# Hyperbolic attention and FP8 feed-forward: a register for the exponential's scale, a small exponential one slot later, and another order of VectorE's steps

## The chip, the cores and the metric

One core of a Trainium2 chip runs the whole layer. The metric is the device time of one execution in microseconds, the median of several runs. TensorE multiplies, ScalarE evaluates functions, VectorE does the elementwise work and reads the products out of PSUM, SyncE (SP) issues all transfers in the stretch in question.

## The reference

The input x has 8 sequences of 1024 tokens with 256 features. The first half of the layer is attention with 16 heads of 16 features, whose weights come from distances in the Poincare ball:

```python
q_h, k_h, v_h = exp_map_at_origin(x @ W.T per head, c)
diff = |q|^2 - 2 q.k + |k|^2
denom = max((1 - c |q|^2) * (1 - c |k|^2), EPS)
dist = arccosh(max(1 + 2 c diff / denom, 1 + EPS)) / sqrt(c)
weights = softmax(-beta_pos * dist - attention_bias)
out = weights @ log_map_at_origin(v_h)      # then exp map, log map, @ W_o.T, + x
```

The second half normalises the sum, quantises it to FP8 (e4m3), multiplies by a 256x256 matrix, adds a bias and adds the result to the sum.

## The kernel before

**Tiles.** The 8192 tokens are 16 groups (`NG`) of 512 queries. A group takes 32 steps: 4 sets of four heads (`HG`) by 8 blocks of 128 keys (`KT`). That makes N = 512 steps, written out without loops. A step is four heads x 128 keys x 512 queries, a tile of 128x2048. In units of four steps (`UNIT`) the kernel chooses between two forms by a flag that it has computed on the chip: closed or open. All engines but TensorE and SP branch on it at each unit's start (L912 to L920, L1008 to L1018). An open unit is one in which the bound of `denom` can be above EPS; the inputs give three open units, which begin at steps 164, 276 and 492.

**A step, closed.** TensorE writes the distances of step n+1 to four PSUM banks (`distances`, in two halves; the tiles of successive steps share two banks, so the second half waits for `freed`). ScalarE takes the logarithm of the four banks into `U` (`log`, L881), which frees the banks, and then the exponential of the step before in place (`power`, L888), whose scale is `g.NEGB`, a column of 128 equal values in SBUF. TensorE multiplies it with the values of its keys (`values`, PSUM bank 6, summed over 8 steps), two steps after the distances. `U` has four slots (`RING`).

**A step, open.** VectorE first writes the bound into `U` (`bound`, L941, four instructions of 128x512), multiplies it with the distances from PSUM (`clamp`, L950, 128x2048, signals `freed`), and ScalarE takes the logarithm of `U` in place (L876). VectorE does the product of step n at the head of step n and the bound of step n+1 behind it; only then follow its copies and slot work of step n.

**Bank 7.** All other matmuls share one PSUM bank in a fixed order (`Uses`): each use waits until VectorE has copied the one before (`b7_copied`), each copy waits for its matmuls (`b7_filled`). Projections of later groups (`PROJECT_USES`: X transposes of the input, M the projection to q, k and v, R transposes of the finished rows, A a maximum for the flag) and the finish of earlier ones (`FINISH_USES`: T, W the output projection, Q, Y the FP8 product) have slots; slot k of the projection is step k - 4 of a group, slot k of the finish is step k. A use marked BOTH is divided: TensorE does one half before `values` of the step and one behind; its copy is in the second half of the step (`in_step(G, s, 1)`). Step 3 to 9 and 11 of a group have M0 to M7; 12 and 13 have T0 and T1, 14 and 15 have W0 and W1. S (step 2, 10, 18, 26) transposes the sums. In a step without a use TensorE does two products for nothing (`keep_busy`, L833). At the end of 8 steps VectorE copies bank 6 to `OTs` (`copy_sums`, L956) and signals `ot_done`, for which the next `values` that starts a sum waits.

**Slot work.** `project.vector` and `finish.vector` are VectorE's elementwise work by slot, at the end of a step. Slot 18 ends with `nrm` (L446). ScalarE's part of it is one small exponential over 128x128 (L407 to L410), now at slot 19: it waits for `n_rdy` and stands behind `log(n)` and `power(n - 1)` of step 15, the last of a unit. Slot 20 of VectorE begins with a wait for its result (`e_rdy`); at step 16 `copy_sums` stands ahead of it. The first two groups are projected before the steps begin, the third from step 0 on, so the steps hold 14 such exponentials.

Each engine's order is the order of the code. TensorE in step n: second half of `distances(n + 1)`, first half of `distances(n + 2)`, uses, `values(n - 1)`, uses.

Of the kernel before, what the change touches and what calls it, by code (L numbers as in the profile page):

```python
# [7 lines left out]
ACT = mybir.ActivationFunctionType  # L8
# [3 lines left out]
I32 = mybir.dt.int32  # L12
# [29 lines left out]
UNIT = 4  # L42
RING = 4
# [50 lines left out]
def hold(eng, passed):  # L94
    eng.sem_inc(passed, 1)
# [167 lines left out]
def at(table, slot, half):  # L263

    return [key for key, where in table.items() if where == (slot, half) or (half, where) == (1, (slot, BOTH))]
# [13 lines left out]
def project_stage(nc, ctx, g, a, uses):  # L279
# [125 lines left out]
            v.sem_inc(a.open_rdy, 1)  # L405

    def scalar(act, n, k):  # L407
        if k == 19:
            act.wait_ge(n_rdy, n + 1)
            act.activation(e[:, :, :], nrm[:, :, :], ACT.Exp, scale=g.M2SC).then_inc(e_rdy, 1)  # L410

# [231 lines left out]
def emit_layer(nc, g):  # L643

    with ExitStack() as ctx:
        def sb(name, shape, dt=F32):
            return _sb(nc, ctx, name, shape, dt)
# [7 lines left out]
        U = sb("U", [P, RING, HPG, GTOK])  # L655
# [14 lines left out]
        def in_step(G, s, half):  # L670

            found = []
            if s % KT == SUM_STEPS % KT and half == 0:
                x = HG * G + (s - SUM_STEPS) // KT
                if 0 <= x < NG * HG and G < NG:
                    found.append(("S", x // HG, x % HG))
            found += [(kind, n, i) for n, k in finished(G, s) for kind, i in at(FINISH_USES, k, half)]
            found += [(kind, n, i) for n, k in projected(G, s) for kind, i in at(PROJECT_USES, k, half)]
            return found

        def projected(G, s):

            return [(n, k) for n, k in ((G + 2, s + EARLY), (G + 3, s + EARLY - STEPS))
                    if n < NG and 0 <= k < PROJECT_SLOTS]

        def finished(G, s):

            return [(n, k) for n, k in ((G - 2, s + STEPS), (G - 1, s)) if n >= 0 and 0 <= k < FINISH_SLOTS]
# [4 lines left out]
        def before_steps(k):  # L693

            return [(n, k - lag) for n, lag in enumerate(LAGS) if 0 <= k - lag < PROJECT_SLOTS]
# [27 lines left out]
        def split(n):  # L723

            return n // STEPS, (n % STEPS) // KT, n % KT
# [5 lines left out]
        def place(n, h):  # L731

            return (h + 2) % HPG if n % 2 else h

        def chunk(n):
            return g.ps[:, 2 * (n % 2):2 * (n % 2) + 4, :].rearrange("p b n -> p (b n)")

        def opened(n):

            G, hg, kt = split(n)  # L740
            return (G * 2 + kt // UNIT) * HG + hg

        def flags_of(n):

            G, hg, kt = split(n)
            return max(G, 2 * (G // 2) + kt // UNIT) + 1

        with nc.Block() as block:
# [120 lines left out]
            @block.scalar  # L869
            def _(act):  # L870
                act.preload_act_table_set(ACT_SET)

                def log(n, is_open):
                    if is_open:
                        act.wait_ge(freed, n + 1)
                        act.activation(U[:, n % RING], U[:, n % RING], ACT.Ln, scale=-2.0, bias=1.0).then_inc(ln_open, 1)  # L876
                    else:
                        act.wait_ge(d_rdy, n + 1)
                        if n >= RING:
                            act.wait_ge(pv_done, n - RING + 1)  # L880
                        act.activation(U[:, n % RING].rearrange("p b n -> p (b n)"), chunk(n), ACT.Ln,  # L881
                                       scale=-2.0 / EPS, bias=1.0).then_inc(freed, 1)

                def power(n, *logs):

                    for done in logs:
                        act.wait_ge(done, n + 1)
                    act.activation(U[:, n % RING], U[:, n % RING], ACT.Exp, scale=g.NEGB).then_inc(exp_done, 1)  # L888

                def unit(n0, is_open):  # L890
                    if is_open:
                        if n0:
                            power(n0 - 1, freed, ln_open)
                    for n in range(n0, n0 + UNIT):
                        G, s = n // STEPS, n % STEPS
                        if is_open and n > n0:
                            power(n - 1, ln_open)
                        log(n, is_open)
                        if not is_open and n > n0:
                            power(n - 1, freed)  # L900
                        elif not is_open:
                            if n0:
                                power(n0 - 1, freed, ln_open)
                            act.sem_inc(ln_open, UNIT)
                        for m, k in projected(G, s):
                            project.scalar(act, m, k)

                act.activation(past[:, :], g.NEGB, ACT.Exp, scale=math.log(2.0 * U_EXACT + 1.0)).then_inc(past_rdy, 1)
                for k in range(LEAD):
                    for n, slot in before_steps(k):  # L910
                        project.scalar(act, n, slot)
                for n0 in range(0, N, UNIT):  # L912
                    o = opened(n0)
                    act.wait_ge(a.open_rdy, flags_of(n0))
                    hold(act, passed_act)
                    is_open = act.value_load(a.opens[0:1, o:o + 1], min_val=0, max_val=1)
                    with act.If(is_open > 0):
                        unit(n0, True)
                    with act.Else():
                        unit(n0, False)  # L920
                power(N - 1, freed, ln_open)

            @block.vector
            def _(v):
# [10 lines left out]
                def bound(n):  # L935

                    G, hg, kt = split(n)
                    if n >= RING:
                        v.wait_ge(pv_done, n - RING + 1)
                    for h in range(HPG):  # L940
                        ins = v.tensor_scalar(U[:, n % RING, place(n, h), :], rqb[:, h, :],  # L941
                                              a.rk[:, (G // 2) % 2, hg * HPG + h, kt:kt + 1],
                                              1.0 / EPS, ALU.mult, ALU.min)
                    ins.then_inc(m_rdy, 1)

                def clamp(n):
                    v.wait_ge(m_rdy, n + 1)
                    v.wait_ge(d_rdy, n + 1)
                    all4 = U[:, n % RING].rearrange("p b n -> p (b n)")
                    v.tensor_tensor(all4, all4, chunk(n), ALU.mult).then_inc(freed, 1)  # L950
# [25 lines left out]
                def copy(kind, n, i):  # L976
                    if kind == "S":
                        normalise(n, i)
                    elif (kind, i) in FINISH_USES:
                        finish.copy(v, n, (kind, i))  # L980
                    else:
                        project.copy(v, n, (kind, i))

                def unit(n0, is_open):
                    for n in range(n0, n0 + UNIT):
                        G, s = n // STEPS, n % STEPS
                        if is_open:
                            clamp(n)
                            if n + 1 < n0 + UNIT:
                                bound(n + 1)  # L990
                        for key in in_step(G, s, 0):
                            copy(*key)
                        if n % KT == 0 and n >= KT:
                            copy_sums(n // KT - 1)
                        for key in in_step(G, s, 1):
                            copy(*key)
                        for m, k in finished(G, s):
                            finish.vector(v, m, k)
                        for m, k in projected(G, s):
                            project.vector(v, m, k)  # L1000
# [7 lines left out]
                for n0 in range(0, N, UNIT):  # L1008
                    o = opened(n0)
                    v.wait_ge(a.open_rdy, flags_of(n0))  # L1010
                    hold(v, passed_v)
                    is_open = v.value_load(a.opens[0:1, o:o + 1], min_val=0, max_val=1)
                    with v.If(is_open > 0):
                        v.wait_ge(rqb_in, 16 * (n0 // KT + 1))
                        bound(n0)
                        unit(n0, True)
                    with v.Else():
                        v.sem_inc(m_rdy, UNIT)  # L1018
                        unit(n0, False)
# [266 lines left out]
```

## Time and profile before

| | us |
|---|---|
| median of 3 runs | 2226.95 |
| the three runs | 2231.99, 2209.66, 2226.95 |
| the profiled execution | 2226.39 |
| its span, first to last instruction | 2224.1 |
| TensorE busy | 1855.3 |
| ScalarE busy | 1896.5 |
| VectorE busy | 1172.3 |

The mean granted TensorE clock is 0.951 of 2.4 GHz. The profile comes from one execution; its own time lies 0.6 us under the median. Successive instructions of an engine can overlap a little, so the pitch (start to start) is the measure of what an instruction costs in a row of others; the duration is longer. Ends of matmuls are modelled. The last group of stretches holds the three open units up to the second closed step behind each, and 11 us around a step 17. In the rows, PE is TensorE, ACT is ScalarE, DVE is VectorE; a bracket gives the idle time of the engine before the instruction and what ended it.

### The profile page before, as it was taken

The page shows a single profiled execution, that of the slowest core. Times are in us where ns is not written, and L with a number is a line of the kernel's source. Part 1 is how long each engine was busy: PE and PEld are TensorE (multiplying, and loading weights), DVE is VectorE, ACT ScalarE, POOL GpSimd, SP SyncE. Part 2 cuts the span into 40 slices and gives each one's busy share as a digit, 9 for nine tenths or more (in the row PEclk, how much of TensorE's full clock was granted, in tenths as well). Part 3 has the DMA queues.
Part 4 walks back from the last instruction along what each step waited for, and adds up shares of the span by engine and source line. Part 5 has one row for each costly group of instructions (what it writes and reads, how often), then busy time and mean ns, then how long its engine had stood idle before and what let it go on. Part 6 is the DMA issues. An engine that isn't in the chain of part 4 may idle for free. (4 is left out here: it accounts for less than half of the span.)

```text
span 2224.1 us, 29561 instructions
## 1 busy us (share of the span) xinstructions
PE 1855.3 (83%) x10721; PEld 617.0 (28%) x10721; DVE 1172.3 (53%) x2869; ACT 1896.5 (85%) x1055; POOL 2.6 (0%) x15
## 2 busy tenths in 40 slices
PE   4459898998989859898989789898989898899792
PEld 2222222232322213222222222222222223233221
DVE  5563345555555545556555655555565555423335
ACT  1019999989999949999999699999999999999790
POOL 0000000000000000000000000000000000000000
PEclk9969999989999969999999899999999999999895
DMA  1031220313131211312213031312213031311000
GB/s 40 22 111 48 80 69 20 120 39 120 39 101 39 99 40 39 103 37 91 67 56 103 19 120 39 101 39 91 67 39 115 25 110 39 110 39 58 20 20 30
DMA packets 112937, 142.54 MB, mean 64 GB/s; under 512 B 35676, under 2 KB 61533, under 8 KB 112733
## 3 DMA queue, kind: packets, MB, share of 16 engines
q1 hardware_dynamic: 112732, 140.13, 20.1%
q8 instruction: 90, 1.47, 0.3%
q14 instruction: 115, 0.93, 0.2%
HBM read 85.07 MB, written 55.05 MB: 63 GB/s over the span
## 5 line engine op out<-in xcount | busy, mean ns | idle before, releaser
L888 ACT ACTIVATE U<-U,sc 128x2048 f32<-128x2048 f32 x512 | 1047.6, 2048 | 0.3
L881 ACT ACTIVATE U<-ps 128x2048 f32<-128x2048 f32 x500 | 959.8, 1920 | 63.6 <-PE ps L797 57.7
L797 PE MATMUL ps<-q_T,k_T 18*128 18x512 f32 x4096 | 638.8, 655 | 183.3 <-ACT U L881 132.7
L810 PE MATMUL ps<-U,vals 128*32 128x512 f32 x4096 | 564.9, 624 | 50.3 <-ACT U L888 42.6
L797 PEld LDWEIGHTS ps<-q_T,k_T 18*128 18x128 f32 x4096 | 200.4, 188 | 406.5 <-ACT U L881 318.1
L347 PE MATMUL ps<-wT,xnT 128*128 128x384 f32 x512 | 247.8, 574 | 17.1 <-DVE qkv L373 14.3
L373 DVE COPY qkv<-ps 128x384 f32<-128x384 f32 x128 | 71.3, 557 | 260.0 <-PE ps L347 259.9
L833 PE MATMUL ps<-woT,ident 128*128 128x256 f32 x428 | 157.9, 452 | 0.0
L956 DVE COPY OTs<-ps 128x512 f32<-128x512 f32 x64 | 44.3, 692 | 194.9 <-PE ps L810 173.4
L352 PE MATMUL ps<-ident,rows 128*128 128x128 f32 x512 | 110.3, 315 | 44.1 <-DVE rows L482 29.8
L347 PEld LDWEIGHTS ps<-wT,xnT 128*128 128x128 f32 x512 | 83.9, 202 | 222.9 <-issue 119.7
L810 PEld LDWEIGHTS ps<-U,vals 128*32 128x32 f32 x4096 | 81.6, 109 | 228.9 <-ACT U L888 192.1
L410 ACT ACTIVATE e<-nrm,sc 128x128 f32<-128x128 f32 x16 | 6.4, 402 | 140.7 <-DVE nrm L446 140.7
L833 PEld LDWEIGHTS ps<-woT,ident 128*128 128x128 f32 x428 | 67.0, 197 | 184.4 <-issue 177.6
L352 PEld LDWEIGHTS ps<-ident,rows 128*128 128x128 f32 x512 | 57.1, 150 | 210.2 <-issue 148.3
L381 DVE COPY q_T<-ps 128x512 f32<-128x512 f32 x64 | 44.1, 690 | 108.0 <-PE ps L352 107.8
L383 DVE COPY k_T<-ps 128x512 f32<-128x512 f32 x64 | 44.3, 692 | 86.0 <-PE ps L352 85.9
L546 PE MATMUL ps<-woT,fi_ocT 128*128 128x256 f32 x256 | 78.1, 432 | 1.6 <-DVE fi_ocT L568 0.8
L876 ACT ACTIVATE U<-U 128x2048 f32<-128x2048 f32 x12 | 22.9, 1912 | 58.8 <-DVE U L950 58.8
L964 DVE TENSOR_REDUCE den<-ps 128x16 f32<-128x256 f32 x64 | 27.2, 425 | 87.0 <-PE ps L819 86.5
L546 PEld LDWEIGHTS ps<-woT,fi_ocT 128*128 128x128 f32 x256 | 47.3, 205 | 58.4 <-issue 29.8
L438 DVE TENSOR_REDUCE ss<-sqr 128x48 f32<-128x768 f32 x64 | 61.0, 953 | 2.2
(164 smaller groups left out, 1168.9 us busy)
## 6 DMA issues: line engine op xcount, KB each, us to landing
rqb<-q_scratch SPq DMA_DIRECT2D x64, 1024.0 KB, 5.6
q_scratch<-q_T SPq DMA_DIRECT2D x16, 1024.0 KB, 4.5
k_scratch<-k_T SPq DMA_DIRECT2D x16, 1024.0 KB, 6.8
v_scratch<-vals SPq DMA_DIRECT2D x16, 768.0 KB, 9.2
xt<-in_L_attn_x_dram SPq DMA_DIRECT2D x16, 512.0 KB, 6.2
fi_xt<-in_L_attn_x_dram SPq DMA_DIRECT2D x16, 512.0 KB, 5.7
out_dram<-fi_x SPq DMA_DIRECT2D x16, 512.0 KB, 4.1
rk_scratch<-rk SPq DMA_DIRECT2D x16, 32.0 KB, 11.9
```

Of the source, the lines that this page charges most:

```text
L347: ins = pe.matmul(bank[:, 0:384], xnT[:, dc, t * P:(t + 1) * P], g.wT[:, dc, half * 384:(half + 1) * 384], start=dc == 0, stop=dc == 1)
L352: ins = pe.transpose(bank[:, t * P:(t + 1) * P], rows[:, qk, t, hg * HPG:(hg + 1) * HPG, :].rearrange("p h r -> p (h r)"), g.ident[:, :])
L373: v.tensor_copy(qkv[:, t, 24 * half:24 * (half + 1), :].rearrange("p h d -> p (h d)"), bank[:, 0:384]).then_inc(a.b7_copied, 1)
L383: v.tensor_copy(a.k_T[:, b % 2, hg, u * GTOK:(u + 1) * GTOK], bank).then_inc(a.b7_copied, 1)
L438: step(v.tensor_reduce(ss[:, t, :], sqr[:, :].rearrange("p (h d) -> p h d", d=DH), AX.X, ALU.add))
L546: ins = pe.matmul(bank[:, a * D:(a + 1) * D], ocT[:, dc, t * P:(t + 1) * P], g.woT[:, dc, :], start=dc == 0, stop=dc == 1)
L797: ins = pe.matmul(g.ps[:, 2 * pair + i, :], a.k_T[HB * h:HB * h + RD, b % 2, hg, kt * P:(kt + 1) * P], a.q_T[HB * h:HB * h + RD, G % 3, hg ...
L810: ins = pe.matmul(g.ps[HB * h:HB * h + VW, 6, :], a.vals[:, b % 2, kt, (hg * HPG + h) // 2, DH * (h % 2):DH * (h % 2) + VW], U[:, n % RING ...
L833: pe.matmul(g.ps[:, 7, 0:D], g.ident[:, :], g.woT[:, 0, :], start=True, stop=True)
L881: act.activation(U[:, n % RING].rearrange("p b n -> p (b n)"), chunk(n), ACT.Ln, scale=-2.0 / EPS, bias=1.0).then_inc(freed, 1)
L888: act.activation(U[:, n % RING], U[:, n % RING], ACT.Exp, scale=g.NEGB).then_inc(exp_done, 1)
L956: v.tensor_copy(OTs[:, :], g.ps[:, 6, :]).then_inc(ot_done, 1)
```

## The change

It does four things. The small exponential moves from slot 19 to slot 20, in ScalarE's order one `log` and one `power` later. The scale of the large exponential is loaded once into a register of ScalarE and given to the instruction from there, instead of as a column of SBUF. In an open unit VectorE does bound and product of step n+1 at the head of step n, ahead of all copies and slot work of step n; the first product of the unit stands in front of the loop. In every unit `copy_sums` moves behind the copies of the second half of the step. One branch of ScalarE's `unit` is written otherwise and gives the same order.

```diff
--- before.py
+++ after.py
@@ -405,7 +405,7 @@
             v.sem_inc(a.open_rdy, 1)
 
     def scalar(act, n, k):
-        if k == 19:
+        if k == 20:
             act.wait_ge(n_rdy, n + 1)
             act.activation(e[:, :, :], nrm[:, :, :], ACT.Exp, scale=g.M2SC).then_inc(e_rdy, 1)
 
@@ -869,6 +869,8 @@
             @block.scalar
             def _(act):
                 act.preload_act_table_set(ACT_SET)
+                exponent = act.alloc_register("exponent")
+                act.reg_load(exponent, g.NEGB[0:1, :].bitcast(I32))
 
                 def log(n, is_open):
                     if is_open:
@@ -885,12 +887,11 @@
 
                     for done in logs:
                         act.wait_ge(done, n + 1)
-                    act.activation(U[:, n % RING], U[:, n % RING], ACT.Exp, scale=g.NEGB).then_inc(exp_done, 1)
+                    act.activation(U[:, n % RING], U[:, n % RING], ACT.Exp, scale=exponent).then_inc(exp_done, 1)
 
                 def unit(n0, is_open):
-                    if is_open:
-                        if n0:
-                            power(n0 - 1, freed, ln_open)
+                    if is_open and n0:
+                        power(n0 - 1, freed, ln_open)
                     for n in range(n0, n0 + UNIT):
                         G, s = n // STEPS, n % STEPS
                         if is_open and n > n0:
@@ -898,7 +899,7 @@
                         log(n, is_open)
                         if not is_open and n > n0:
                             power(n - 1, freed)
-                        elif not is_open:
+                        if not is_open and n == n0:
                             if n0:
                                 power(n0 - 1, freed, ln_open)
                             act.sem_inc(ln_open, UNIT)
@@ -984,16 +985,15 @@
                 def unit(n0, is_open):
                     for n in range(n0, n0 + UNIT):
                         G, s = n // STEPS, n % STEPS
-                        if is_open:
-                            clamp(n)
-                            if n + 1 < n0 + UNIT:
-                                bound(n + 1)
+                        if is_open and n + 1 < n0 + UNIT:
+                            bound(n + 1)
+                            clamp(n + 1)
                         for key in in_step(G, s, 0):
+                            copy(*key)
+                        for key in in_step(G, s, 1):
                             copy(*key)
                         if n % KT == 0 and n >= KT:
                             copy_sums(n // KT - 1)
-                        for key in in_step(G, s, 1):
-                            copy(*key)
                         for m, k in finished(G, s):
                             finish.vector(v, m, k)
                         for m, k in projected(G, s):
@@ -1013,6 +1013,7 @@
                     with v.If(is_open > 0):
                         v.wait_ge(rqb_in, 16 * (n0 // KT + 1))
                         bound(n0)
+                        clamp(n0)
                         unit(n0, True)
                     with v.Else():
                         v.sem_inc(m_rdy, UNIT)
```

## Rows read from the trace of the kernel before

**Rows 1.** The page, part 1: busy time of each engine over the span.
```profile
PE 1855.3 (83%) x10721; PEld 617.0 (28%) x10721; DVE 1172.3 (53%) x2869; ACT 1896.5 (85%) x1055; POOL 2.6 (0%) x15
```

**Rows 2.** Line 881, the closed logarithm: ns min/median/max, first and last start in us.
```profile
L881 ACT ACTIVATE U<-ps x500: 1864/1906/2072, 156.1 to 2163.1; 128x2048 f32<-128x2048 f32 x167
```

**Rows 3.** The waits: waiting line, releaser: us in total, times, longest.
```profile
ACT e L410 <- DVE nrm L446: 140.7, 15, 57.2
...
ACT U L881 <- PE ps L797: 57.7, 39, 27.2
```

**Rows 4.** Timeline of a plain step: start, us, engine, line, what.
```profile
1003.03 1.87 ACT L881 ACTIVATE U<-ps 128x2048 f32<-128x2048 f32 x1
...
1004.79 2.00 ACT L888 ACTIVATE U<-U,sc 128x2048 f32<-128x2048 f32 x1
...
1004.96 1.24 PE L797 MATMUL ps<-q_T,k_T 18*128 18x512 f32 x8
...
1006.13 0.70 PE L833 MATMUL ps<-woT,ident 128*128 128x256 f32 x2
...
1006.68 1.87 ACT L881 ACTIVATE U<-ps 128x2048 f32<-128x2048 f32 x1
```

**Rows 5.** Timeline, steps 7 to 9 of a group, with projection matmuls.
```profile
1579.20 1.14 PE L797 MATMUL ps<-q_T,k_T 18*128 18x512 f32 x8
...
1582.95 1.14 PE L797 MATMUL ps<-q_T,k_T 18*128 18x512 f32 x8
...
1584.13 1.88 ACT L881 ACTIVATE U<-ps 128x2048 f32<-128x2048 f32 x1
...
1587.18 0.69 DVE L956 COPY OTs<-ps 128x512 f32<-128x512 f32 x1 [1.64 <-PE ps L347]
...
1588.40 0.91 PE L347 MATMUL ps<-wT,xnT 128*128 128x384 f32 x2 [0.55 <-DVE qkv L373]
```

**Rows 6.** Timeline around the small exponential, steps 14 to 16 of that group.
```profile
1608.62 2.02 ACT L888 ACTIVATE U<-U,sc 128x2048 f32<-128x2048 f32 x1
...
1609.44 1.14 PE L797 MATMUL ps<-q_T,k_T 18*128 18x512 f32 x8
...
1612.57 1.13 PE L546 MATMUL ps<-woT,fi_ocT 128*128 128x256 f32 x4
1612.89 0.40 ACT L410 ACTIVATE e<-nrm,sc 128x128 f32<-128x128 f32 x1 [2.24 <-DVE nrm L446]
1613.72 1.88 ACT L881 ACTIVATE U<-ps 128x2048 f32<-128x2048 f32 x1 [0.43 <-issue]
...
1618.68 0.69 DVE L956 COPY OTs<-ps 128x512 f32<-128x512 f32 x1 [2.47 <-PE ps L810]
```

**Rows 7.** Stretches: length, busy us (count) of PE, PEld, DVE, ACT, POOL, then clock, DMA, GB/s.
```profile
791.30:834.80 43.50, 28.56 (x89) 7.42 (x89) 19.84 (x36) 17.41 (x9) 0.00 (x0) 0.59 0.08 24
1251.20:1281.50 30.30, 20.86 (x90) 6.30 (x91) 19.53 (x45) 17.42 (x9) 0.00 (x0) 0.68 0.11 35
2079.30:2111.90 32.60, 23.57 (x97) 8.47 (x97) 14.15 (x20) 17.42 (x9) 0.00 (x0) 0.74 0.10 33
341.00:352.00 11.00, 10.98 (x52) 3.27 (x52) 4.76 (x13) 9.07 (x6) 0.00 (x0) 0.69 0.01 1
```

**Rows 8.** Timeline, the first two steps of the first open unit.
```profile
791.24 1.67 DVE L941 TENSOR_SCALAR U<-rqb,rk 128x512 f32<-128x512 f32 x4
...
791.38 2.19 PE L797 MATMUL ps<-q_T,k_T 18*128 18x512 f32 x8 [6.93 <-DVE U L950]
...
798.63 0.56 DVE L373 COPY qkv<-ps 128x384 f32<-128x384 f32 x1 [5.72 <-PE ps L347]
...
800.58 2.29 DVE L950 TENSOR_TENSOR U<-U,ps 128x2048 f32<-128x2048 f32 x1
...
802.90 1.91 ACT L876 ACTIVATE U<-U 128x2048 f32<-128x2048 f32 x1 [7.60 <-DVE U L950]
...
804.84 2.00 ACT L888 ACTIVATE U<-U,sc 128x2048 f32<-128x2048 f32 x1
```

## The prediction

> **What bounds the kernel now.** I read the costliest groups, then the waits, then ScalarE's timeline. ScalarE does 512 steps of one logarithm and one exponential over 128x2048 and is busy 1,896.5 of 2,224.1 us; TensorE's 1,855.3 hold modelled ends and are read from its starts below [rows 1]. In a plain step the logarithm starts 1.76 us before the exponential and the exponential 1.89 us before the next logarithm: 3.65 us a step, with no idle time [rows 4]. TensorE is second: it starts the distances 0.06 us after the logarithm ends and could have had them ready 1.18 us after their start [rows 5], where the next logarithm comes 1.72 us after it [rows 4]. That is 0.54 us of slack.
>
> From the first closed logarithm (156.1) to the last (2163.1) [rows 2] 511 steps would take 1,865 us at 3.65; they take 2,007. The 142 us beyond that stand in four places, and the change touches all: (a) ScalarE waits for `nrm` ahead of the small exponential, 140.7 us, of which 111.6 are the two waits of 54.4 and 57.2 before the steps begin and 29.1 are thirteen waits of 2.24 [rows 3, 6]; (b) behind them TensorE, left idle 2 us, falls to its 1.2 GHz level (granted clock 0.69 in 341 to 352) and delays later logarithms [rows 7]; (c) some tenths in each stretch with the projection's matmuls [rows 5]; (d) three open units, 12 steps: with the wait ahead of each and the step behind it 70 us beyond 3.65 a step, 43.5, 30.3 and 32.6 us for nine activations each [rows 7].
>
> **The change, part by part.**
>
> *Scale out of a register.* The exponential loses its per-partition operand. Nowhere does the trace show an activation scaled from a register. The nearest row is the open logarithm: same tile, same memory, same width, both constants immediate: 1.91 against 2.00 us for the exponential right behind it [rows 8]. So 0.09 less. The bounds: nothing saved (0), or the whole difference between the closed logarithm's 1.76 and the exponential's 1.89, 0.13 [rows 4]; but the closed one reads PSUM, so I take 0.09. The new step is 3.56. The one register load is a single instruction before the loops, hidden in the 54 us in which ScalarE idles there, one of its first two waits [rows 3]. How many steps gain? Of 511: minus 8 in each of 14 groups (TensorE bound, below), 4 in each of 13 (counted below), 12 around two open units, 3 at the start: 332 x 0.09 = 30 us.
> The Trainium skill (ScalarE: Activation LUTs, What ACT_TABLE_LOAD costs) gives 93 ns for each pointer operand and 186 ns + 0.833 ns a column with an overlap of 93 ns otherwise, which is an estimated pitch of 1.80, not the logarithm's 1.76. By it the 0.13 bound is out and the term is 31 us; with 0.13 it would be 43.
>
> *Steps with projection matmuls (s = 3 to 9).* TensorE runs from distances to distances in 3.75 us (1579.20 to 1582.95) [rows 5], slower than ScalarE at either price, so nothing of the register is earned here. Seven such steps from a distance start 1.93 us behind a logarithm's start, and 1.18 to the next: 1.93 + 26.25 + 1.18 = 29.36 us for eight steps. Now they take about 30.0: 29.2, 0.2 of such stalls and 0.6, because at s = 8 VectorE copies `OTs` (0.69 us) before the projection's bank and TensorE waits 0.55 for it [rows 5]. The order copy, then `copy_sums`, removes this: the bank is copied at 1587.2, `OTs` by 1588.3, and the product that needs `ot_done` starts a half use (0.91 busy, some 0.84 from start to start) after 1587.8. The other places where the order turns (s = 0, 24) have no stall to lose: the sums come 0.7 later, and TensorE has its distances (1.17) and a half use to do before. 13 groups x 0.64 = 8 us.
>
> *Small exponential at slot 20 (s = 16).* `nrm` comes 2.24 us too late for its present place; the new place is one logarithm and one exponential later, 3.56 us. Margin 1.3. Behind the waiting instruction stood the whole queue: 0.40 for itself and 0.43 until the next logarithm, because the unit's flag load and branch had been held up too [rows 6]; from exponential to logarithm 5.10 instead of 1.89, so 3.21 us. VectorE, who now waits for `e` at slot 20, is covered: at s = 16 it first copies `OTs`, which waits for TensorE's product of the step before and idles 2.47 us [rows 6]; `e` is done about 2 us before that copy ends. Without that cover VectorE would wait some 2 us, five steps before TensorE uses the rows that it prepares.
> But the wait also hid TensorE. Steps 14 and 15 carry the output projection: 1609.44 to 1612.57 and 1.06 more (the last half use, 1.13 busy) is 4.19 us each [rows 6]. With step 14's logarithm at 0: distances start at 1.93, 6.12, 10.31, and, after a step with keep-busy products (0.70 busy for the projection's 0.91 [rows 4, 5]: 0.21 less in each half than 3.75, so 3.33), 13.64. Logarithm 16 at 7.30 (ScalarE alone 7.11), 17 at 11.49 (alone 11.15 with the small exponential, which thus costs nothing), 18 at 15.05, ScalarE's own time again. Now: 14.6 + 3.21 = 17.81. Gain 2.76 x 13 = 36 us. This is what is late next: TensorE takes 0.8 of the 3.2 back.
>
> *TensorE's clock.* With the 2 us of idle gone I expect no fall behind it. Its price: of the 57.7 us in which the closed logarithm waits for distances, 27.2 are the first; about 7 are the 0.6 at s = 8, 6.5 stand behind open units, 1.7 in the first steps; 15 are left, most of them one or two steps behind the small exponential [rows 3]. 15 us.
>
> *Open units.* Now each step is a chain: product (2.29), distances, half use, values, half use, copy of the bank, slot work (the 1.4 us to 800.58), next product: 11.5 us from the first open logarithm to the second, mostly at 1.2 GHz (distances 2.19 for 1.24) [rows 4, 8]. Behind the change the next bound (1.67) and product stand before the copies. The product frees its banks; TensorE needs 2.12 for distances, so in the first unit the second logarithm comes 4.7 us after the first (2.2 + 2.3 + 0.2). Then the bank's copy must be waited for, which TensorE allows 7.25 us after it starts the distances (791.38 to 798.63) [rows 8]; copy 0.5, slot work 1.4, bound 1.7, product 2.2 and 0.1: 13.2. The same again, with 7.2 us of TensorE and about 1.9 us of slot work (two passes over 128x768) of the next slot: 21.0. The closed logarithm is at 23.8 and the next, with a bank copy still owed, at 31.0, where now it is 43.5 [rows 7]: 12.5. In the same way the second (projection's transposes, short) goes from 30.3 to 25.0 and the third (two transposes, little slot work) from 32.6 to 18.7 [rows 7]. Together 32 us. Bounds: 12 if the deferred copies stall TensorE afterwards at its low clock, 42 if the higher clock holds. No DMA is moved; SP's `rqb` load waits for `m_rdy`, which comes earlier.
>
> Sum: 30 + 8 + 36 + 15 + 32 = 121. Against this execution's 2226.4 (median 2226.95) that is **2105 us**.
>
> **Rivals.**
> 1. *The register buys nothing* (it is expanded to an operand, or its fetch costs the same). For it: no row shows it. Then 30 fewer: 2135. Chance 0.12.
> 2. *The open units give little*: VectorE's total per open step is the same, only deferred, and the debt is paid in the next closed steps at low clock. Then 12 for 32, or less: 2125 to 2137. Chance 0.08.
> 3. *Slower: the register ends ScalarE's run-ahead.* If an activation with a register can be issued only when the one before is finished, each exponential shows a gap like the 0.43 us at 1613.72 [rows 6]. 512 x 0.43 = 220 against 91 for all but the register: 2355. It decides from 0.18 us an exponential on. Against it: flag load and branch, also register work, are normally hidden behind an activation. Chance 0.04.
> 4. *The moves give back what they take* (VectorE late for `e`, or TensorE bound from s = 14 on with its clock still falling, and no gain from the open units): 36 + 15 + 32 shrink to under 20, and with rival 1 the time is 2205 to 2225. Chance 0.03.
> The remaining 0.73 is my forecast with its own range 2088 to 2125.
>
> **Numbers.** 2105 is the likeliest. The low end, 2084: 0.13 for 0.09 (-12) and open units at 42 (-10). The high end, 2140, takes in rivals 1 and 2. A measurement of this kernel can tell about 1% (22 us; its three runs lie between 2209.66 and 2231.99). Faster by over 1%: 0.73 + 0.12 + 0.08 = 0.93; within 1%: 0.03; slower: 0.04.
>
> **What would show it.** Exponential at about 1.91 beside an open logarithm, pitch 3.56 in plain steps; no idle time in front of the small exponential after the first two, and 0.2 to 0.5 us of idle before the logarithms 16 and 17; granted clock near 1 in the stretch behind; `OTs` copied after the bank at s = 8 and no 0.6 us stall; open logarithms 5 to 8 us apart. The forecast falls if the pitch stays 3.65 or grows, if VectorE idles for `e`, or if the steps behind an open unit are longer by more than the unit got shorter.

## The result, and the profile after

The changed kernel takes 2101.22 us (median of 4 runs, 2090.92 to 2106.49), the kernel before 2218.68 (4 runs, the three shown and one more at 2210.42): ratio 0.946, 95% interval 0.939 to 0.953. The profiled execution took 2098.05 us, span 2096.3. The forecast was 2105, range 2084 to 2140.

The busy times and the two large lines of ScalarE in the page after (as in [rows 1]; lines behind 873 are one or two higher than before):

```profile
PE 1805.1 (86%) x10721; PEld 604.4 (29%) x10721; DVE 1171.7 (56%) x2869; ACT 1853.0 (88%) x1055; POOL 2.6 (0%) x15
...
L883 ACT ACTIVATE U<-ps 128x2048 f32<-128x2048 f32 x500 | 963.8, 1928 | 48.1 <-PE ps L797 40.8
L890 ACT ACTIVATE U<-U 128x2048 f32<-128x2048 f32 x512 | 1004.6, 1964 | 0.3
```

ScalarE is busy 1853 us, 43.5 less. Its exponential's mean duration is 1964 ns and no longer carries `sc` among its inputs; before it was 2048. The closed logarithm is what it was.

The waits of ScalarE in the profile after (as in [rows 3]):

```profile
ACT e L410 <- DVE nrm L446: 105.7, 2, 59.0
...
ACT U L883 <- PE ps L797: 40.8, 24, 27.2
ACT U L878 <- DVE U L951: 26.9, 10, 7.3
```

The small exponential waits twice instead of 15 times; the two are those before the steps begin. Its thirteen waits are gone, and no row of VectorE waiting for ScalarE has taken their place. ScalarE's waits for an open product fell to 26.9 us; before they were 58.8, in 12 waits.

The step without projection, timeline after (as in [rows 4]):

```profile
1440.35 1.94 ACT L883 ACTIVATE U<-ps 128x2048 f32<-128x2048 f32 x1
...
1442.11 1.98 ACT L890 ACTIVATE U<-U 128x2048 f32<-128x2048 f32 x1
...
1442.35 1.24 PE L797 MATMUL ps<-q_T,k_T 18*128 18x512 f32 x8 [0.70 <-ACT U L883]
...
1443.91 1.95 ACT L883 ACTIVATE U<-ps 128x2048 f32<-128x2048 f32 x1
```

Logarithm to exponential 1.76 us as before, exponential to logarithm 1.80 instead of 1.89; the step is 3.56 instead of 3.65.

The eighth step of the same group as in [rows 5], timeline after:

```profile
1489.73 1.14 PE L797 MATMUL ps<-q_T,k_T 18*128 18x512 f32 x8
...
1493.49 1.14 PE L797 MATMUL ps<-q_T,k_T 18*128 18x512 f32 x8
1493.60 0.56 DVE L373 COPY qkv<-ps 128x384 f32<-128x384 f32 x1 [1.28 <-PE ps L347]
1494.08 0.68 DVE L957 COPY OTs<-ps 128x512 f32<-128x512 f32 x1
...
1494.56 0.91 PE L347 MATMUL ps<-wT,xnT 128*128 128x384 f32 x2
1494.66 1.88 ACT L883 ACTIVATE U<-ps 128x2048 f32<-128x2048 f32 x1
```

`OTs` now follows the bank's copy, TensorE starts the projection's next half 1.07 us after the distances and waits for nothing. Distances still come every 3.75 us (1489.73 to 1493.49): this stretch is TensorE's.

The steps 14 to 17 of that group, timeline after (as in [rows 6]):

```profile
1509.10 1.89 ACT L883 ACTIVATE U<-ps 128x2048 f32<-128x2048 f32 x1
...
1511.04 1.24 PE L797 MATMUL ps<-q_T,k_T 18*128 18x512 f32 x8 [0.33 <-ACT U L883]
...
1515.33 1.14 PE L797 MATMUL ps<-q_T,k_T 18*128 18x512 f32 x8
...
1516.50 1.88 ACT L883 ACTIVATE U<-ps 128x2048 f32<-128x2048 f32 x1
...
1518.44 0.29 DVE L446 TENSOR_TENSOR nrm<-ss,y 128x128 f32<-128x128 f32 x1
...
1519.52 1.14 PE L797 MATMUL ps<-q_T,k_T 18*128 18x512 f32 x8
...
1520.08 0.39 ACT L410 ACTIVATE e<-nrm,sc 128x128 f32<-128x128 f32 x1
...
1520.69 1.88 ACT L883 ACTIVATE U<-ps 128x2048 f32<-128x2048 f32 x1 [0.22 <-PE ps L797]
...
1522.35 0.69 DVE L957 COPY OTs<-ps 128x512 f32<-128x512 f32 x1 [0.25 <-PE ps L810]
...
1522.84 1.14 PE L797 MATMUL ps<-q_T,k_T 18*128 18x512 f32 x8
1522.96 0.22 DVE L460 TENSOR_SCALAR rp<-e 128x128 f32<-128x128 f32 x1
...
1524.27 1.87 ACT L883 ACTIVATE U<-ps 128x2048 f32<-128x2048 f32 x1
```

`nrm` is ready at 1518.73, the small exponential starts at 1520.08 with no idle time: 1.35 us of margin. The distances start at 1511.04, 1515.33, 1519.52 and 1522.84, the logarithms 14, 16, 17 and 18 at 1509.10, 1516.50, 1520.69 and 1524.27. VectorE's first use of `e` is at 1522.96, right behind the copy of `OTs`, 2.5 us after `e` was ready.

The open units up to the second closed step behind each, and 11 us from step 17 on of the group in which before was at 1.2 GHz for a time (columns as in [rows 7]):

```profile
759.70:784.80 25.10, 22.76 (x89) 6.21 (x90) 19.93 (x36) 17.05 (x10) 0.00 (x0) 0.73 0.14 42
1178.50:1201.10 22.60, 18.36 (x90) 5.21 (x91) 20.12 (x45) 16.98 (x10) 0.00 (x0) 0.75 0.16 47
1967.10:1987.60 20.50, 18.57 (x97) 6.63 (x98) 14.28 (x19) 17.08 (x10) 0.00 (x0) 0.83 0.19 53
337.00:348.00 11.00, 10.22 (x65) 3.62 (x68) 9.36 (x27) 11.00 (x7) 0.00 (x0) 1.00 0.07 26
```

The units take 25.1, 22.6 and 20.5 us, where they took 43.5, 30.3 and 32.6. The last stretch has a granted clock of 1.00, where it was 0.69; in the steps 16 to 19 it is 1.00 in all 14 groups with a small exponential.

The first open unit, timeline after (as in [rows 8]):

```profile
759.73 1.91 ACT L878 ACTIVATE U<-U 128x2048 f32<-128x2048 f32 x1 [7.29 <-DVE U L951]
...
759.75 2.19 PE L797 MATMUL ps<-q_T,k_T 18*128 18x512 f32 x8 [6.93 <-DVE U L951]
...
761.95 2.29 DVE L951 TENSOR_TENSOR U<-U,ps 128x2048 f32<-128x2048 f32 x1 [0.66 <-PE ps L797]
...
764.27 1.91 ACT L878 ACTIVATE U<-U 128x2048 f32<-128x2048 f32 x1 [0.69 <-DVE U L951]
...
766.71 1.14 PE L797 MATMUL ps<-q_T,k_T 18*128 18x512 f32 x8
766.82 0.56 DVE L373 COPY qkv<-ps 128x384 f32<-128x384 f32 x1 [2.58 <-PE ps L347]
...
772.80 1.91 ACT L878 ACTIVATE U<-U 128x2048 f32<-128x2048 f32 x1 [4.67 <-DVE U L951]
```

The second product starts 2.22 us behind the first logarithm (759.73 to 761.95), as soon as the distances are there (VectorE idles 0.66 us), and the second open logarithm comes after 4.54 us instead of 11.5. The third comes 8.53 us after it, behind the deferred copy and slot work.

Where the 120 us of the stepping part went, worked out from the starts of the logarithms in both traces (from the first closed one to the last: 2007.0 and 1887.2 us):

| | before | after | less |
|---|---|---|---|
| steps 3 to 10, mean of 12 groups | 30.07 | 29.60 | 0.47 |
| steps 14 to 19, mean of 12 groups | 26.42 | 22.28 | 4.14 |
| a plain step | 3.65 | 3.56 | 0.09 |
| three open units, entry not counted | 106.3 | 68.0 | 38.3 |

The 12 groups are 1 to 13 without the one that has an open unit in the steps in question or right behind them. Times 13, the first two rows are 6.1 and 53.8 us; with the units that is 98.2. The rest of the 119.8 is the shorter step elsewhere, about 26 us, less 4.8 us that the steps 0 to 10 of group 0 took longer in this execution (47.2 instead of 42.4 us): TensorE was at 1.2 GHz for the first 22 us of them, before for the first 12. From step 11 of group 0 on, the stepping part fell by 124.5 us. The end of step 10 of group 0 lies between 189 and 205 us in the executions traced here, whatever the variant; what sets it was not tried. So a single trace is compared below from step 11 on as well.

### The profile page after: what moved, and what is told of

Same layout as the page of the kernel before. It is cut to its first block and busy times, and to the rows that moved or that the text cites. A ratio compares the mean times of both kernels' runs of the same rounds, so it can differ in the third digit from the quotient of the medians.

```text
span 2096.3 us, 29568 instructions
## 1 busy us (share of the span) xinstructions
PE 1805.1 (86%) x10721; PEld 604.4 (29%) x10721; DVE 1171.7 (56%) x2869; ACT 1853.0 (88%) x1055; POOL 2.6 (0%) x15
## 5 line engine op out<-in xcount | busy, mean ns | idle before, releaser
L890 ACT ACTIVATE U<-U 128x2048 f32<-128x2048 f32 x512 | 1004.6, 1964 | 0.3
L797 PE MATMUL ps<-q_T,k_T 18*128 18x512 f32 x4096 | 627.7, 645 | 133.4 <-ACT U L883 107.6
L810 PE MATMUL ps<-U,vals 128*32 128x512 f32 x4096 | 555.0, 614 | 27.9 <-ACT U L890 27.6
L347 PE MATMUL ps<-wT,xnT 128*128 128x384 f32 x512 | 239.7, 557 | 11.4 <-DVE qkv L373 8.7
L833 PE MATMUL ps<-woT,ident 128*128 128x256 f32 x428 | 151.2, 435 | 0.0
L437 DVE TENSOR_TENSOR sqr<-qkv 128x768 f32<-128x768 f32 x64 | 60.7, 949 | 0.9 <-DVE qkv L373 0.8
```

Source lines behind the costliest of these rows:

```text
L347: ins = pe.matmul(bank[:, 0:384], xnT[:, dc, t * P:(t + 1) * P], g.wT[:, dc, half * 384:(half + 1) * 384], start=dc == 0, stop=dc == 1)
L437: step(v.tensor_tensor(sqr[:, :], src, src, ALU.mult))
L797: ins = pe.matmul(g.ps[:, 2 * pair + i, :], a.k_T[HB * h:HB * h + RD, b % 2, hg, kt * P:(kt + 1) * P], a.q_T[HB * h:HB * h + RD, G % 3, hg ...
L810: ins = pe.matmul(g.ps[HB * h:HB * h + VW, 6, :], a.vals[:, b % 2, kt, (hg * HPG + h) // 2, DH * (h % 2):DH * (h % 2) + VW], U[:, n % RING ...
L833: pe.matmul(g.ps[:, 7, 0:D], g.ident[:, :], g.woT[:, 0, :], start=True, stop=True)
```

## The experiments

Each part alone in the kernel before; then three of them undone in the changed kernel, all but the open order. Ratios are against the kernel before on the same chip.

**1. The register alone** (`b_register`).

```diff
+                exponent = act.alloc_register("exponent")
+                act.reg_load(exponent, g.NEGB[0:1, :].bitcast(I32))
...
-                    act.activation(U[:, n % RING], U[:, n % RING], ACT.Exp, scale=g.NEGB).then_inc(exp_done, 1)
+                    act.activation(U[:, n % RING], U[:, n % RING], ACT.Exp, scale=exponent).then_inc(exp_done, 1)
```

> The kernel before with the large exponential's scale out of a register, nothing else. Theory of the forecast: exponential to logarithm 1.80 instead of 1.89 us, but only the steps that ScalarE bounds gain: about 332 x 0.09 = 30 us, because the steps with projection matmuls stay at TensorE's 3.75 and the wait for nrm (set by TensorE and VectorE) grows by what ScalarE arrives earlier; so 13 waits of 2.24 become 2.3 to 3. Rival, plain arithmetic: every one of 512 gains 0.09, 46 us.

Ratio 0.992 (0.989 to 0.995), 2200.75 for 2222.06 us: 21 less; the stepping part 21.9 less (21.7 from step 11 on). The pitch is 3.56 as expected, and plain arithmetic (46) is out. It is less than 30; two waits grew. Waits of ScalarE in this kernel's profile, and one of the waits for `nrm` from its timeline:

```profile
ACT e L410 <- DVE nrm L446: 134.9, 15, 55.4
ACT U L883 <- PE ps L797: 68.3, 44, 27.2
```

```profile
326.01 0.40 ACT L410 ACTIVATE e<-nrm,sc 128x128 f32<-128x128 f32 x1 [2.42 <-DVE nrm L446]
```

The wait for `nrm` is 2.42 in each of 13 groups where it was 2.24; the row's total is under the 140.7 of before only because one of the two waits ahead of the steps was 48.0 us instead of 54.4. The logarithms wait 68.3 us for distances instead of 57.7: the falls of TensorE's clock behind the wait cost more in this execution (steps 14 to 17 took 19.36 us instead of 18.65). The granted clock was under 1 in the steps 16 to 19 of all 12 groups counted, in the kernel before in 9 of 12. Whether the register does that, or the execution, one trace can't tell.

**2. The slot alone** (`b_slot20`).

```diff
-        if k == 19:
+        if k == 20:
             act.wait_ge(n_rdy, n + 1)
```

> The kernel before with the small exponential at slot 20, nothing else. Theory: the 13 waits of 2.24 us and the 0.43 behind them go, TensorE gives back about 0.5 a group in the output projection's steps: 13 x 2.7 = 35 us, and its clock no longer falls behind them: 15 us more, 50 in all; VectorE does not idle for e. Rival: the wait goes over to VectorE, which then waits for e and delays the bank's copies: under 15 us.

Ratio 0.980 (0.975 to 0.985), 2176.84: 45 less; the stepping part 48.0 less. The thirteen waits are gone (111.6 us in 2 waits are left), no wait of VectorE for `e` has come, and the steps 14 to 19 take 22.55 us in each of the 12 groups counted, where before they took 25.1 to 29.4. The rival is out.

**3. The open order alone** (`b_open_order`).

```diff
-                        if is_open:
-                            clamp(n)
-                            if n + 1 < n0 + UNIT:
-                                bound(n + 1)
+                        if is_open and n + 1 < n0 + UNIT:
+                            bound(n + 1)
+                            clamp(n + 1)
...
                         bound(n0)
+                        clamp(n0)
                         unit(n0, True)
```

> The kernel before with the product of the next step ahead of the copies in open units, nothing else. Theory: 32 to 36 us, all of it in three units, where open logarithms come 4 to 9 us apart instead of 6 to 12. Rival: the copies put off stall TensorE in the next closed steps, about 12 us net.

Ratio 0.979 (0.974 to 0.983), 2177.39: 45 less; the stepping part 41.4 less (43.3 from step 11 on), of it about 38 in the three units; most of the rest is TensorE's clock, which fell in 8 of the 12 groups instead of 9 and cost 0.36 us a group less. The steps behind the units became no longer: 2.14 and 6.02 us behind the first, where they were 2.14 and 6.04. So the deferred copies were not paid back by TensorE.

**4. The sums' copy alone** (`b_sums_behind`).

```diff
-                        if n % KT == 0 and n >= KT:
-                            copy_sums(n // KT - 1)
                         for key in in_step(G, s, 1):
                             copy(*key)
+                        if n % KT == 0 and n >= KT:
+                            copy_sums(n // KT - 1)
```

> The kernel before with the sums' copy behind the bank's copy, nothing else. Theory: the stall of 0.6 us at step 8 of each group with projection matmuls goes, the eight steps from 3 to 11 shrink from 30.0 to about 29.4 us: 8 us, too little for the times, so the trace decides. Rival: the product that needs the sums' copy waits instead and the eight steps keep their 30.0 us.

Ratio 1.000 (0.997 to 1.004). The times tell nothing, as expected. In the trace the steps 3 to 10 take 29.56 us instead of 30.07: 0.5 a group, some 7 us. The stall went and did not move to the product that needs the sums' copy.

**5. The column back, in the changed kernel** (`a_column`): experiment 1 the other way.

> The changed kernel with the column of SBUF as scale again. Theory of the forecast: 30 us slower than the changed kernel (about 2131 us), exponential to logarithm 1.89 again. Rival, plain arithmetic over 512 steps: 46 us slower.

2125.31 us, ratio 0.957 (0.954 to 0.960): 24 above the changed kernel's median and 26 above experiment 6 on the same chip. The stepping part is 27.4 longer, although group 0 had no slow start here (42.0 us for its steps 0 to 10 instead of 47.2); from step 11 on it is 32.6 longer, of which 2.0 are in the second open unit, at a lower clock. So in the trace the register is worth some 31 us, the 30 of the forecast, and 9 more than in experiment 1, where the longer wait for `nrm` (13 x 0.18 us) and the clock behind it take some of it back. The times alone are too coarse to tell the two experiments apart. The steps 3 to 10 (29.57) and 14 to 17 (15.25 for 15.16) hardly differ, which is why it is not 46.

**6. The scale as a number** (`a_constant`).

```diff
+NEG_BETA = -math.sqrt(math.log(2.0))
...
-                    act.activation(U[:, n % RING], U[:, n % RING], ACT.Exp, scale=exponent).then_inc(exp_done, 1)
+                    act.activation(U[:, n % RING], U[:, n % RING], ACT.Exp, scale=NEG_BETA).then_inc(exp_done, 1)
```

> The changed kernel with the scale as a number written into the instruction (the value that the inputs give), the register gone. Theory: a register costs what an immediate costs, so pitch 1.80 and the changed kernel's time within 0.5%. Rival: resolving the register takes part of the 0.13 us that the closed logarithm is ahead (1.76 against 1.89), then the pitch falls below 1.80, towards 1.76, and the time by up to 14 us.

2098.83 us, ratio 0.946 (0.943 to 0.949), the changed kernel's own; the stepping part 1885.6 for 1887.2 us, the step 3.56. A register costs ScalarE what an immediate costs. The 0.04 us by which the closed logarithm's pitch (1.76) is shorter still is not the register's; what it is (the logarithm reads PSUM, the exponential SBUF) was argued, not tried.

**7. The slot back, in the changed kernel** (`a_slot19`): experiment 2 the other way.

> The changed kernel with the small exponential back at slot 19. Theory: waits for nrm of 2.3 us or more come back in 13 groups, ScalarE idles, TensorE's clock falls behind most of them: 45 to 55 us slower, about 2150. Rival: the other parts have moved nrm forward, so that the wait is short and under 20 us come back.

2155.87 us, ratio 0.970 (0.967 to 0.973): 55 above the changed kernel, the stepping part 50.5 longer (55.6 from step 11 on); 13 waits for `nrm` are back, 2.42 us each, and steps 14 to 17 take 18.92 us instead of 15.16.

**8. TensorE kept busy during the wait, in the kernel before** (`b_filled`).

```diff
+PROJECT_FILL = 15
...
+                    if s == PROJECT_FILL and G + 2 < NG:
+                        for _ in range(3):
+                            keep_busy(first_use[n + 1])
```

> The kernel before, with three more products for nothing on TensorE at the end of step 15 of the 13 groups in question (as keep_busy does them; they wait for the bank's copy), while ScalarE waits for nrm as before. Theory: TensorE's fall to 1.2 GHz is caused by the 2 us of idle behind the wait; with the idle cut to about 1 us the logarithms of steps 17 to 19 lose their stalls of 0.7 to 2.6 us: about 15 us faster, the wait for nrm unchanged at 2.24. Rival: the fall has another cause; it stays and the time is the same.

Ratio 0.992 (0.990 to 0.995), 2207.18 for 2225.07: 18 less. The wait and the start of the three products in the timeline:

```profile
328.00 0.40 ACT L411 ACTIVATE e<-nrm,sc 128x128 f32<-128x128 f32 x1 [2.24 <-DVE nrm L447]
328.84 1.88 ACT L885 ACTIVATE U<-ps 128x2048 f32<-128x2048 f32 x1 [0.44 <-issue]
...
329.59 1.56 PE L834 MATMUL ps<-woT,ident 128*128 128x256 f32 x6 [0.78 <-DVE fi_x L575]
...
331.08 1.14 PE L798 MATMUL ps<-q_T,k_T 18*128 18x512 f32 x8
```

And the stretch from step 17 on, as the last of [rows 7]:

```profile
332.00:343.00 11.00, 10.14 (x65) 3.40 (x61) 7.11 (x23) 11.00 (x7) 0.00 (x0) 1.00 0.01 1
```

The wait is 2.24 us as before, and TensorE stands idle 0.78 us instead of 1.95; the granted clock stays at 1.00 in the steps 16 to 19 of every group. The edit also puts the three products into group 0, which has no wait; there they make the six steps 0.35 us longer. The steps 14 to 19 take 25.1 us in eleven of the 12 groups counted and 25.4 in one, where the kernel before had a mean of 26.42 and a spread of 4.3: 1.3 x 13 = 17 us (16.6 less in the stepping part from step 11 on). So the fall is caused by the idle time behind the wait, and it had a price of its own, apart from the wait. The same count splits the slot's gain: 16 to 17 us of clock and (25.12 - 22.55) x 13 = 33 us of waiting.

**9. The sums' copy in front again, in the changed kernel** (`a_sums_first`), experiment 4 the other way, seen once in the trace.

> The changed kernel with the sums' copy in front of the bank's copy again. Theory: the 0.6 us stall at step 8 comes back on top of a TensorE that is already the bound there: steps 3 to 10 from 29.6 to 30.2 us, 8 us in all. Rival: it was hidden by the faster ScalarE's other waits, and the eight steps stay at 29.6.

The one execution took 2115.96 us, 17.9 more than the changed kernel's profiled one. Most of that is not the price of the copy: the first logarithm alone comes 10.3 us later (160.5 for 150.2). From step 11 on the stepping part is 7.7 us longer, of which 1.7 are in the first open unit and 6.0 in the steps 3 to 10: those take 30.06 us instead of 29.60, 0.46 a group more, not quite 0.6. Its eighth step in the timeline, against the one shown above:

```profile
1509.17 0.69 DVE L957 COPY OTs<-ps 128x512 f32<-128x512 f32 x1 [1.35 <-PE ps L347]
1509.78 0.55 DVE L373 COPY qkv<-ps 128x384 f32<-128x384 f32 x1
...
1510.38 0.91 PE L347 MATMUL ps<-wT,xnT 128*128 128x384 f32 x2 [0.26 <-DVE qkv L373]
```

`OTs` is in front again, and TensorE's half use starts 0.26 us late in this group.

**10 and 11. Two attempts at what is left.** ScalarE's stalls of a group are now 1.1 us in the seven projection steps in a row and 0.9 in the two output projection steps. Only the entries of the two tables that change are shown.

```diff
 v_w_apart:
-("W", 1): (15, BOTH)
+("W", 1): (16, BOTH)
 v_spread:
-("M", 3): (10, BOTH), ("M", 4): (11, BOTH), ("M", 5): (12, BOTH), ("M", 6): (13, BOTH), ("M", 7): (15, BOTH)
+("M", 3): (11, BOTH), ("M", 4): (12, BOTH), ("M", 5): (13, BOTH), ("M", 6): (15, BOTH), ("M", 7): (16, BOTH)
-("T", 0): (12, BOTH), ("T", 1): (13, BOTH), ("W", 0): (14, BOTH), ("W", 1): (15, BOTH)
+("T", 0): (13, BOTH), ("T", 1): (14, BOTH), ("W", 0): (15, BOTH), ("W", 1): (17, BOTH)
```

> The changed kernel with only the second output projection use one slot later (16), so that a light step stands between the two. Theory: TensorE is late by 0.2 to 0.3 us once or twice instead of 0.93 in all; the four steps 14 to 17 shrink from 15.16 to about 14.7 us, 14 x 0.5 = 7 us. Rival: step 16 is where the small exponential stands and the sums are copied, and its 0.29 us, free in TensorE's shade so far, now counts: the four steps stay within 0.15 us of 15.16.

> The changed kernel with the uses of bank 7 spread: the projection's matmuls at slots 7, 8, 9 and 11, 12, 13 and 15, 16 (steps 3 to 5, 7 to 9, 11, 12), the finish's T at 13 and 14, W at 15 and 17. What is left of ScalarE's stalls in a group is now 1.1 us in the seven projection steps in a row (3.75 each) and 0.9 in the two adjacent output projection steps (4.19 each). Theory: a light step between lets ScalarE and TensorE's slack of 0.45 us come back; about 0.9 us of 2.0 stays, so 14 x 1.1 = 16 us faster than the changed kernel, about 2085. Rival: VectorE, whose slot work now follows the copies more closely at step 12, brings nrm late or delays the bank, and the gain is under 5 us.

`v_w_apart` has 2094.93 us (ratio 0.942, 0.939 to 0.945), `v_spread` 2096.57 (0.944, 0.941 to 0.947): neither can be told from the changed kernel's 0.946. In the trace a plain group shrank from 115.9 to 115.7 and to 115.4 us, 0.2 and 0.5 instead of the expected 0.5 and 1.1. In `v_w_apart` the steps 14 to 17 went from 15.16 only to 14.91. In `v_spread` they went to 14.54, but a part of it is lost at step 18; its timeline there:

```profile
1516.47 1.88 ACT L883 ACTIVATE U<-ps 128x2048 f32<-128x2048 f32 x1
...
1520.03 0.41 ACT L410 ACTIVATE e<-nrm,sc 128x128 f32<-128x128 f32 x1
...
1520.32 1.88 ACT L883 ACTIVATE U<-ps 128x2048 f32<-128x2048 f32 x1
...
1522.44 1.14 PE L797 MATMUL ps<-q_T,k_T 18*128 18x512 f32 x8
...
1523.51 1.13 PE L546 MATMUL ps<-woT,fi_ocT 128*128 128x256 f32 x4
...
1523.88 1.89 ACT L883 ACTIVATE U<-ps 128x2048 f32<-128x2048 f32 x1
...
1525.57 1.13 PE L546 MATMUL ps<-woT,fi_ocT 128*128 128x256 f32 x4
...
1526.63 1.14 PE L797 MATMUL ps<-q_T,k_T 18*128 18x512 f32 x8
...
1527.81 1.88 ACT L883 ACTIVATE U<-ps 128x2048 f32<-128x2048 f32 x1 [0.24 <-PE ps L797]
```

The step that took over the second output projection use is now the long one for TensorE: with both halves (1.13 each) its distances come 4.19 us apart (1522.44 to 1526.63), and the logarithm waits for them and comes 3.93 us after the one before. VectorE isn't what delays it: its copy of that use waited 2.06 us for TensorE. The small exponential also costs its 0.29 us now, no longer in TensorE's shade (1516.47 to 1520.32 is 3.85). In `v_w_apart` the step with the small exponential takes 3.87 us in the same way. Both theories were half right: the slack comes back, but a use costs TensorE the same wherever it stands, and the small exponential's time counts as soon as TensorE no longer covers it. The shorter groups of `v_spread` are also in part offset by its first open unit, 28.1 us instead of 25.0 in this execution.

## Why the prediction was right, point by point

- **Scale out of a register, 30 us.** Right: some 31 in the changed kernel (5), 22 alone (1). The price of 0.09 per exponential was taken from the open logarithm's row and is what the pitch shows (1.80 for 1.89). That only some 330 of 511 steps earn it is shown by both experiments: 46 us appear in neither. The interaction with the wait for `nrm` is not in the prediction; only the expectation of experiment 1 has it.
- **Projection steps, 8 us.** The stall behind `OTs` went as forecast, 0.5 a group (4, 9). The eight steps take 29.60, not 29.36: the distances start 2.07 us behind the logarithm of step 3 (1468.81 to 1470.88 in the group shown), not 1.93, since the logarithms last 2.01 us there and not the 1.87 of the row that I used, and the first of the seven intervals is 3.85 (1470.88 to 1474.73). So 6 to 7 us instead of 8.
- **Small exponential, 36 us.** Right in mechanism, 3 us high: 33 us (2, 8). Distances were forecast at 1.93, 6.12, 10.31 and 13.64 behind the logarithm of step 14 and came at 1.94, 6.23, 10.42 and 13.74; the logarithms 16 to 18 at 7.30, 11.49, 15.05 and came at 7.40, 11.59, 15.17. The loss ahead of it was forecast exactly (17.81 for the steps 14 to 17, 17.84 in experiment 8). That TensorE takes back 0.8 us (it was 0.9), that `e` costs nothing there, and that the copy of `OTs` covers VectorE is what the trace shows.
- **TensorE's clock, 15 us.** Right: 17 us by experiment 8, which leaves the wait and takes only the idle time away.
- **Open units, 32 us.** Right in mechanism, low in size: 38.3, in the changed kernel and alone. The forecast kept TensorE at 1.2 GHz through the first unit; in the trace it is at 2.4 for a time (granted clock 0.50 in 759.7 to 766.4, 0.99 in 766.4 to 773.2, 0.51 in 773.2 to 780.1; at 766.71 the distances take 1.14, at 759.75 2.19). Ahead of that rise it had worked without idle time from 759.75 on, where in the kernel before it stood idle 4.3 to 5.7 us ahead of the distances of each later open step; that this is the reason was not tried. That unit took 25.0 us from the first open logarithm on, forecast 31.0; the second 22.5, forecast 25.0; the third 20.5, forecast 18.7, with TensorE at the low clock again on the way (granted clock 0.50 in 1978.2 to 1981.6).
- **The rivals.** The register buys nothing: out by 1 and 5. The open units give little: out by 3. The register ends ScalarE's run-ahead: out by the 1.80 and by 6. The moves give back what they take: out by 2 and 7.

The five terms were 121; the stepping part fell by 119.8, the profiled execution by 128.3, the medians by 117.5. The difference stands outside: the first logarithm starts at 150.2 instead of 156.1 and the end is 2.1 us shorter. Measured one by one the terms are about 31, 6, 33, 17 and 38: 125, which is what the trace shows from step 11 of group 0 on (124.5). The forecast was 6 us low in the open units and about 5 high in the second and third term, so the sum is closer than its terms. That it also meets the median (2105 for 2101) has some luck in it: the 121 were taken from one execution of 2226.4, which lies 8 us above the median of 2218.7 that the kernel before had with its fourth run.

## What to carry to other kernels

A wait in a queue costs more than its length: here 2.24 us of waiting cost 0.4 for the instruction, 0.4 of idle time behind it (by the order of the code the unit's branch, held up too; not tried apart), and 1.3 us more for the matmul clock that the idle neighbour lost; and it hides 0.9 us of another engine's deficit, which is what remains when it is gone. Price a shorter instruction only in the steps that its engine bounds, and ask which wait swallows it: by the traces the register was worth 22 us beside the wait and some 31 without. In a chain that runs over three engines, put first the instruction that frees a bank for the others, and the copies behind it.

## What the runs showed of the hardware

An activation whose scale comes from a sequencer register has the pitch of one with an immediate, 1.80 us at 128x2048 with the tile in SBUF, against 1.89 with a per-partition column; the difference is what the Trainium skill gives for a pointer operand (ScalarE: Activation LUTs, What ACT_TABLE_LOAD costs) (93 ns), and the pitch is the 1.80 estimated from that page ahead of the result. For the closed logarithm, which reads PSUM, that estimate is 0.04 too long: its pitch is 1.76. TensorE's granted clock fell to 1.2 GHz behind 1.95 to 2.25 us of idle time in 9 of 12 groups, and in none behind 0.78 us: its price varied from 0 to 4.3 us a group in one execution. That this is part of why the kernel before scatters is likely, but not shown.
